# The reciprocal root of three layer normalisations as a power on GpSimd

## The chip, the cores and the metric

The kernel runs on one core of one Trainium2 chip. The metric is the device time of one execution in microseconds (us). The profile is of one more execution, taken by the hardware profiler; its times in the rows are us from the start of its span.

## The reference

The input x has shape 4 x 512 x 128 in float32, 2048 tokens of 128 features. Four blocks follow each other, each with a layer normalisation ahead of it and a residual addition behind it:

```
def _layernorm(x, axis=-1, eps=1e-05):
    m = jnp.mean(x, axis=axis, keepdims=True)
    v = jnp.var(x, axis=axis, keepdims=True)
    return (x - m) / jnp.sqrt(v + eps)

x = x + attn_a(_layernorm(x), ...)   # inner training, two steps
x = x + ffn(_layernorm(x), ...)      # mixture of 8 experts, the best 2
x = x + attn_b(_layernorm(x), ...)   # 16 heads, block-causal, own normalisation on top
x = x + ffn(_layernorm(x), ...)      # the same mixture again
```

In ffn a token's gates are a softmax over 8 logits; the two largest, made to sum to 1, weigh the outputs x We + be of their experts.

## The kernel before

The tokens lie in 16 tiles of 128 (partitions) x 128, all in the SBUF tensor x. The phases run one after the other, each a block in which every engine has an instruction list of its own, tied to the others by semaphores: qkv_phase, two rounds of gradient_phase and schulz_phase, query_phase (together the first block of the reference), moe_phase(0), attention_phase, moe_phase(1). The order on each engine is written out by hand; `pipeline` interleaves stages with a lag between them.

**The layer normalisation** is made for all 16 tiles at once. The statistics of each tile (L176, one instruction a tile) come at the end of the phase before. `ln_vector` on VectorE turns them into a variance plus epsilon in five steps of 128 x 16 (L182 to L186), each waiting for the one before; then it signals (L187), makes the mean in two steps (L188, L189), waits for the root (L190) and takes its reciprocal into rstd (L191). `ln_scalar` on ScalarE loads the Sqrt table (L195), waits for the variance and takes the root (L197). The first phase calls both as well and needs the Sqrt table for other roots too (L283, L306).

**moe_phase.** VectorE: L1138 is the normalisation, L1147 normalises a tile, in groups of four tiles; L1153 copies logits; from L1160 a long serial chain finds the two best gates (L1160, L1161 maximum and shift, L1163 to L1165 softmax, `best` twice, up to L1183, which writes the weights wt). TensorE turns the normalised tiles (L1096), makes logits (L1103) and turns those (L1109), waits for all logits to be copied (L1123), then runs `experts` for the first two tiles, twelve matmuls through `mm3` (L117 to L119, where each matmul's record stands), then in `weights` turns wt (L1115) and makes the twelve matmuls for the experts' biases (again L117 to L119), for which VectorE waits before its four additions to x (L1194, L1197). ScalarE: L1041 is `ln_scalar`; L1047 and L1052 copy tiles and logits; L1065 loads the Exp table; L1061 makes the high parts of the first two tiles, which GpSimd's low parts (L1034) and through them the experts wait for; L1070 is the exponential, which waits for the shifted logits (L1069). GpSimd begins with eight memsets of the priorities (L1014), copies tiles (L1021), makes low parts (L1034), then one half-sum per tile (L1030); VectorE goes on with L1212, L1217 and the addition to x at L1222.

**attention_phase.** ScalarE: L1370 is `ln_scalar`, L1371 loads Exp. GpSimd: memsets of the mask (L1343, L1346), then the bias (L1351). VectorE: L1514 is the normalisation, L1521 normalises four tiles, and TensorE turns them (L1412).

In the first phase GpSimd's list starts with memsets of ones, ident and be (L245, L246, L250); the last of them releases SP's loads of the expert biases (L602).

Of the kernel before, what the change touches and what calls it, by code (L numbers as in the profile page):

```python
# [29 lines left out]
P = 128  # L30
# [91 lines left out]
class Kernel:  # L122
    def __init__(self, nc, ctx, args, out):
        self.nc, self.ctx = nc, ctx
        self.a, self.out = args, out
        sb, ps = self.sb, self.ps
        self.x = sb("x", [P, NT, P])
        self.ident = sb("ident", [P, P])
        self.ones = sb("ones", [P, P])
        self.mean = sb("mean", [P, NT])  # L130
        self.rstd = sb("rstd", [P, NT])
        self.stats = sb("stats", [P, NT, 6])
        self.lnw = sb("lnw", [P, 4, NT])

        self.we = sb("we", [P, NE * P])
        self.weh, self.wel = sb("weh", [P, NE * P], F32R), sb("wel", [P, NE * P], F32R)
        self.wg, self.bg = sb("wg", [P, NE]), sb("bg", [NE, 1])

        self.beh, self.bel = sb("beh", [P, NT * P], F32R), sb("bel", [P, NT * P], F32R)

        self.wh, self.wl = sb("wh", [P, 3 * HEADS * DH], F32R), sb("wl", [P, 3 * HEADS * DH], F32R)
        self.wout, self.bout = sb("wout", [P, NP, P]), sb("bout", [P, 1, P])
        self.lng, self.lnb = sb("lng", [P, 1]), sb("lnb", [P, 1])
        self.s_late, self.s_bias, self.s_parts = self.sem("late"), self.sem("bias"), self.sem("parts")
        self.gradient_sems()
        self.schulz_sems()
# [28 lines left out]

        return e.bn_stats(self.stats[:, bass.ds(tile, 1), :], self.x[:, bass.ds(tile, 1), :])  # L176

    def ln_vector(self, e, s_var, s_root, s_ln):

        st, w = self.stats, self.lnw  # L180
        c = Chain(e, s_ln)
        c(e.tensor_tensor(w[:, 0, :], st[:, :, 1], st[:, :, 4], ALU.subtract))  # L182
        c(e.tensor_tensor(w[:, 1, :], w[:, 0, :], w[:, 0, :], ALU.mult))
        c(e.tensor_tensor(w[:, 2, :], st[:, :, 2], st[:, :, 5], ALU.add))
        c(e.scalar_tensor_tensor(w[:, 3, :], w[:, 1, :], P / 4.0, w[:, 2, :], ALU.mult, ALU.add))
        c(e.tensor_scalar(w[:, 3, :], w[:, 3, :], 1.0 / P, LN_EPS, ALU.mult, ALU.add))  # L186
        e.sem_inc(s_var, 1)  # L187
        c(e.tensor_tensor(w[:, 0, :], st[:, :, 1], st[:, :, 4], ALU.add))  # L188
        c(e.tensor_scalar(self.mean[:, :], w[:, 0, :], 0.5, None, ALU.mult))  # L189
        e.wait_ge(s_root, 1)  # L190
        c(e.reciprocal(self.rstd[:, :], w[:, 1, :]))  # L191
        return c.n

    def ln_scalar(self, e, s_var, s_root):
        e.preload_act_table(ACT.Sqrt)  # L195
# [5 lines left out]
    def qkv_phase(self):  # L201
# [8 lines left out]
        with ExitStack() as c:  # L210
# [32 lines left out]
            @block.gpsimd  # L243
            def _(pool):
                pool.memset(self.ones[:, :], 1.0).then_inc(s_cst, 1)  # L245
                pool.memset(ident[:, :], 0.0).then_inc(s_cst, 1)  # L246
                pool.wait_ge(s_cst, 2)
                pool.affine_select(out=ident[:, :], in_=ident[:, :], compare_op=ALU.not_equal, fill=1.0, base=0,
                                   pattern=[[-1, P]], channel_multiplier=1).then_inc(s_cst, 1)
                pool.memset(self.be[:, :, :], 0.0).then_inc(self.s_bias, 1)  # L250
                pool.wait_ge(s_cst, 3)
                pool.wait_ge(s_unit, 6 * 16)
                g = Chain(pool, s_pre)
                per_head = lambda ap, n: ap[:, n * P:n * P + P].rearrange("p (g d) -> p g d", d=QD)
                for dst, src in ((scale_all, scale), (shift_all, shift_)):
                    for n in range(2):
                        g(pool.tensor_tensor(per_head(dst, n), per_head(self.ones, 0), src[:, n:n + 1, :].broadcast_to([P, QH, QD]), ALU.mult))
                wide = lambda ap: ap.rearrange("p (a d) -> p a d", d=P)
                g(pool.tensor_tensor(wide(self.gvh[:, :]), wide(self.gv[:, :]),
                                     self.ones[:, :].unsqueeze(1).broadcast_to([P, 2 * NC, P]), ALU.mult))  # L260
                g(pool.tensor_tensor(self.gvl[:, :], self.gv[:, :], self.gvh[:, :].bitcast(F32), ALU.subtract))
                pool.wait_ge(s_ptc, 2)
                g(pool.tensor_tensor(self.pTl[:, :], self.projT[:, :], self.pTh[:, :].bitcast(F32), ALU.subtract))
                pool.sem_inc(s_s, 2)
                pool.sem_inc(s_b, 2)

                def unit(t):
                    pool.wait_ge(s_inv, t.done())
                    pool.wait_ge(s_s, t.done())
                    pool.tensor_tensor(m[:, t.ring, :].rearrange("p (g d) -> p g d", d=QD),  # L270
                                       qkv[:, tile(t), 0:2 * P].rearrange("p a (g d) -> p (a g) d", d=QD),
                                       inv[:, heads(t)].unsqueeze(2).broadcast_to([P, 2 * QH, QD]), ALU.mult).then_inc(s_m, 1)

                def scaled(t):
                    pool.wait_ge(s_m, t.done())
                    pool.wait_ge(s_b, t.done())
                    pool.tensor_tensor(sc[:, t.ring, :], m[:, t.ring, :], scale_all[:, :], ALU.mult).then_inc(s_s, 1)

                pipeline(pool, (0, unit), (1, scaled))()
# [66 lines left out]
            @block.vector  # L346
            def _(dve):
                for g in range(BATCH):
                    dve.wait_ge(s_x[g], 16)
                    for n in range(TPB):  # L350
                        self.take_stats(dve, g * TPB + n).then_inc(s_stat, 1)
                dve.wait_ge(s_stat, NT)
                self.ln_vector(dve, s_var, s_root, s_ln)
                dve.scalar_tensor_tensor(nmr[:, :], self.mean[:, :], -1.0, self.rstd[:, :], ALU.mult, ALU.mult).then_inc(s_shift, 1)
                dve.sem_inc(s_xT, 2)
                dve.sem_inc(s_out, 2)
                dve.sem_inc(s_ss, 2)
                dve.sem_inc(s_T, 2)
                dve.wait_ge(s_w, 32)
                dve.wait_ge(s_pre, 4)  # L360

                def bias_add(t):
                    dve.wait_ge(s_qkv, t.done())
                    dve.tensor_tensor(qkv[:, tile(t), :], psQ[t.ring][:, :], bias[:, :], ALU.add).then_inc(s_out, 1)

                def sumsq(t):
                    dve.wait_ge(s_sq, t.done())
                    dve.tensor_reduce(ssq[:, heads(t)], sq[:, t.ring, :].rearrange("p (g d) -> p g d", d=QD),
                                      AX.X, ALU.add).then_inc(s_ss, 1)

                def guard(t):
                    dve.wait_ge(s_rt, t.done())
                    dve.tensor_scalar(ssq[:, heads(t)], ssq[:, heads(t)], 1e-6, None, ALU.add).then_inc(s_gd, 1)

                def invert(t):
                    dve.wait_ge(s_gd, t.done())
                    dve.reciprocal(inv[:, heads(t)], ssq[:, heads(t)]).then_inc(s_inv, 1)

                def shift(t):
                    dve.wait_ge(s_s, t.done() + 2)  # L380
                    dve.wait_ge(s_T, t.done())
                    dve.wait_ge(s_k, t.done())
                    dve.tensor_tensor(u[:, t.ring, :], sc[:, t.ring, :], shift_all[:, :], ALU.add).then_inc(s_b, 1)

                pipeline(dve, (2, bias_add), (3, sumsq), (4, guard), (8, shift), (5, invert))()
# [199 lines left out]
    def load_later_weights(self, sp):  # L585
# [13 lines left out]
        ]  # L599
        for dst, src in loads:  # L600
            sp.dma_start(dst, src).then_inc(self.s_late, 16)
        sp.wait_ge(self.s_bias, 1)  # L602
        for t in range(NT):
            sp.dma_start(self.be[t * NE:(t + 1) * NE, t, :], self.a["L0_ffn_be"]).then_inc(self.s_late, 16)

# [363 lines left out]
    def moe_phase(self, nth):  # L969
# [13 lines left out]
        with ExitStack() as c:  # L983
# [26 lines left out]

            @block.gpsimd
            def _(pool):
                for n in range(NE):
                    last = pool.memset(prio[:, :, n:n + 1], float(NE - n))  # L1014
                last.then_inc(s_prio, 1)
# [22 lines left out]

            @block.scalar
            def _(act):  # L1040
                self.ln_scalar(act, s_var, s_root)  # L1041

                def copy(t):
                    act.wait_ge(s_xT, t.done() + 2)
# [17 lines left out]

                act.sem_inc(s_E, 2)
                act.sem_inc(s_w, 2)
                act.preload_act_table(ACT.Exp)  # L1065
                act.wait_ge(s_keep, 1 + 2)
                for t in FIRST:
                    high(t)
# [201 lines left out]
    def attention_phase(self):  # L1270
# [4 lines left out]
        with ExitStack() as c:  # L1275
# [63 lines left out]

            @block.gpsimd  # L1340
            def _(pool):
                g = Chain(pool, t["cst"])
                g(pool.memset(mask[:, :], 0.0))  # L1343
                for n in range(P // FRAME - 1):
# [22 lines left out]

            @block.scalar
            def _(act):
                self.ln_scalar(act, t["var"], t["root"])  # L1370
                act.preload_act_table(ACT.Exp)  # L1371

                def take_x(b):
# [281 lines left out]
```

## Time and profile before

| | us |
|---|---|
| median of 3 runs | 913.87 (912.15 to 914.26) |
| the profiled execution's own time | 913.51 |
| its span | 911.7 |
| TensorE, matmuls busy | 778.6 (85%) |
| TensorE, weight loads busy | 594.6 (65%) |
| VectorE busy | 600.5 (66%) |
| ScalarE busy | 420.7 (46%) |
| GpSimd busy | 376.6 (41%) |

In the rows PE is TensorE (PEld its weight loads), DVE VectorE, ACT ScalarE, POOL GpSimd, and L12 is line 12 of the kernel. Times at matmuls are modelled: an entry's duration has the pipeline's depth in it, and the spacing of starts tells the rate. A timeline row that stands for several instructions (x4) has the time from the first start to the last end. An idle time in brackets is that of the engine before the row, with what ended it. PEclk is the clock that TensorE was granted, 1.00 for 2.4 GHz and 0.50 for 1.2 GHz. The normalisations of the second, third and fourth block stand at about 406, 476 and 843 us.

### The profile page before, as it was taken

To read this page: it belongs to the slowest core of one execution; us is meant where nothing else is said; L and a number is where in the kernel's file an instruction comes from. 1 tells how busy PE (TensorE), PEld (TensorE's weight loads), DVE (VectorE), ACT (ScalarE), POOL (GpSimd) and SP (SyncE) were. 2 spreads that over 40 slices of the span, in tenths; PEclk is the share of its full clock that TensorE was granted. 3 is DMA by queue.
4 is the path that set the end of the run, shared out by engine and by line. 5 is a ranking of instruction groups with operands and counts; after the bars stand their busy time and mean duration, and the time that the engine had idled before them with its cause. 6 is when DMAs were issued, how large, how long until landed. Compare 5 with 4: busy or idle time off the path is not lost. (4 is left out here: it accounts for less than half of the span.)

```text
span 911.7 us, 16940 instructions
## 1 busy us (share of the span) xinstructions
PE 778.6 (85%) x5464; PEld 594.6 (65%) x5464; DVE 600.5 (66%) x1621; ACT 420.7 (46%) x1190; POOL 376.6 (41%) x512
## 2 busy tenths in 40 slices
PE   3669999879999667968628999999999999998763
PEld 1249999758999656755315766777777777777442
DVE  3936665355655556766996767766676666664698
ACT  4743332433333223314534666565556555562453
POOL 4854443015445534204642443343334333332275
PEclk9979999989999978997987999999999999999798
DMA  3030000000000000000000000000000000000001
GB/s 99 1 128 1 0 0 1 1 0 1 1 0 0 1 0 1 1 1 0 0 0 1 2 1 2 2 1 2 2 1 1 2 1 1 2 1 2 1 12 35
DMA packets 9327, 7.00 MB, mean 8 GB/s; under 512 B 1456, under 2 KB 8880, under 8 KB 9136
## 3 DMA queue, kind: packets, MB, share of 16 engines
q1 hardware_dynamic: 9264, 6.18, 2.1%
q8 instruction: 37, 0.61, 0.3%
q14 instruction: 26, 0.21, 0.1%
HBM read 5.13 MB, written 1.05 MB: 7 GB/s over the span
## 5 line engine op out<-in xcount | busy, mean ns | idle before, releaser
L1356 POOL TENSOR_SCALAR t_p_<-t_p_,t_rinv_ 128x128 f32<-128x128 f32 (+3 forms) x256 | 132.5, 535 | 213.5 <-DVE t_rinv_ L1551 213.5
L1544 DVE CUSTOM_DVE_ANT_0 t_p_<-t_S_,t_mask_ 128x128 f32<-128x128 f32 (+3 forms) x256 | 112.8, 487 | 72.7 <-PE t_S_ L1443 69.2
L1386 ACT ACTIVATE t_p_<-t_p_,t_nmin_ 128x128 f32<-128x128 f32 (+3 forms) x256 | 140.0, 551 | 9.0 <-DVE t_nmin_ L1544 9.0
L1391 ACT ACTIVATE t_pT_<-t_T_ 128x384 f32<-128x384 f32 (+1 forms) x96 | 50.7, 528 | 128.3 <-PE t_T_ L1455 128.3
L1455 PEld LDWEIGHTS t_T_<-ident,t_p_ 128*128 128x128 f32 x640 | 68.3, 140 | 44.6 <-POOL t_p_ L1356 28.7
L1443 PE MATMUL t_S_<-t_k_,t_q_ 64*128 64x256 f32 (+3 forms) x512 | 95.0, 469 | 0.0
L1470 PE MATMUL t_O_<-t_pT_,t_v_ 128*64 128x128 f32 x1280 | 91.0, 280 | 0.1
L1455 PE MATMUL t_T_<-ident,t_p_ 128*128 128x128 f32 x640 | 91.0, 281 | 0.0
L1470 PEld LDWEIGHTS t_O_<-t_pT_,t_v_ 128*64 128x64 f32 x1280 | 67.9, 136 | 29.9 <-ACT t_pT_ L1391 26.5
L432 POOL TENSOR_TENSOR g_sp<-g_s,g_t 128x512 f32<-128x512 f32 x32 | 40.9, 1277 | 103.3 <-DVE g_t L553 103.3
L1555 DVE COPY t_pT_<-t_T_ 128x384 f32<-128x384 f32 (+1 forms) x96 | 57.3, 597 | 3.1 <-PE t_T_ L1455 3.0
L544 DVE TENSOR_TENSOR g_sw<-g_G,g_s 128x512 f32<-128x512 f32 x32 | 22.1, 692 | 55.3 <-ACT g_s L456 55.3
L1030 POOL TENSOR_TENSOR m_z_<-m_y_ 128x512 f32<-128x512 f32 x32 | 43.4, 1355 | 27.9 <-DVE m_y_ L1204 27.9
L117 PE MATMUL m_E_<-weh,m_xh_ 128*128 128x512 f32 x64 | 29.2, 456 | 29.5 <-issue 14.9
L1443 PEld LDWEIGHTS t_S_<-t_k_,t_q_ 64*128 64x128 f32 x512 | 41.3, 185 | 18.9 <-issue 15.8
L1386 ACT ACTIVATION_READ_ACCUMULATOR t_p_<-t_p_,t_nmin_ 128x1 f32 x256 | 48.7, 190 | 0.0
L465 ACT ACTIVATE g_hT<-g_H 128x512 f32<-128x512 f32 x32 | 19.1, 597 | 58.3 <-PE g_H L497 58.3
L438 POOL TENSOR_TENSOR g_w<-g_u,g_sp 128x512 f32<-128x512 f32 x32 | 41.3, 1292 | 3.6 <-POOL g_sp L432 2.2
L1217 DVE TENSOR_TENSOR m_z_<-m_z_ 128x128 f32<-128x128 f32 x32 | 39.6, 1238 | 0.8 <-DVE x L1222 0.5
L117 PEld LDWEIGHTS m_E_<-weh,m_xh_ 128*128 128x128 f32 x64 | 13.0, 204 | 41.3 <-POOL m_xl_ L1034 19.9
L1083 ACT ACTIVATE m_y_<-m_E_,m_wt_ 128x128 f32<-128x128 f32 x128 | 36.4, 368 | 6.0 <-PE m_E_ L119 6.0
L504 PEld LDWEIGHTS g_PT<-proj,g_hT 128*128 128x128 f32 x256 | 33.6, 192 | 2.6
(270 smaller groups left out, 1849.4 us busy)
## 6 DMA issues: line engine op xcount, KB each, us to landing
wqkv<-in_L_attn_b_w_qkv_dram SPq DMA_DIRECT2D x1, 1536.0 KB
x<-in_L_attn_a_x_dram SPq DMA_DIRECT2D x4, 256.0 KB, 4.0
out_dram<-x SPq DMA_DIRECT2D x4, 256.0 KB, 2.3
we<-in_L_ffn_We_dram SPq DMA_DIRECT2D x1, 512.0 KB
wout<-in_L_attn_b_w_out_dram SPq DMA_DIRECT2D x1, 512.0 KB
proj<-n_L_attn_a_ttt_proj_dram SPq DMA_DIRECT2D x1, 256.0 KB, 6.1
gv<-n_L_attn_a_ttt_gate_dram SPq DMA_DIRECT2D x1, 256.0 KB, 5.1
gv<-in_L_attn_a_ttt_val_dram SPq DMA_DIRECT2D x1, 256.0 KB, 5.7
```

What stands on the lines that cost most here:

```text
L117: e.matmul(out, ah, bh, start=start, stop=False)
L432: pool.tensor_tensor(sp_[:, t.ring, :], s_[:, t.ring, :], t1[:, t.ring, :], ALU.subtract).then_inc(g["sp"], 1)
L438: pool.tensor_tensor(w1[:, t.ring, :], u_[:, t.ring, :], sp_[:, t.ring, :], ALU.mult).then_inc(g["w1"], 1)
L1030: pool.tensor_tensor(z[:, t.ring, :], y[:, t.ring, 0:4 * P], y[:, t.ring, 4 * P:8 * P], ALU.add).then_inc(s_z, 1)
L1356: last = pool.tensor_scalar(pr[:, G.par, h, cols], pr[:, G.par, h, cols], rinv[:, G.par, n:n + 1], 1.0, ALU.mult, ALU.mult)
L1386: act.activation(pr[:, G.par, h, cols], pr[:, G.par, h, cols], ACT.Exp, bias=nmin[:, G.par, n:n + 1], scale=-1.0, accum_out=rsum[:, G.par, ...
L1391: act.activation(pT[:, G.par, 0, G.blocks], psT[:, 0, 0:G.width], ACT.Copy).then_inc(t["eA"], 1)
L1443: last = pe.matmul(psS[:, (2 * G.n + h) % 3, at_:at_ + (qt + 1) * P], qp[d, G.par, qt * P:qt * P + P], kp[d, G.par, 0:(qt + 1) * P], start ...
L1455: last = pe.transpose(psT[:, h, k:k + P], pr[:, G.par, h, at_:at_ + P], ident[:, :])
L1470: last = pe.matmul(psO[d, qt * P:qt * P + P], v[:, G.b % 2, n, G.p * P + h * DH:G.p * P + h * DH + DH], pT[:, G.par, h, at_:at_ + P], star ...
L1544: dve.tensor_tensor_reduce(pr[:, G.par, h, cols], psS[:, (2 * G.n + h) % 3, at_:at_ + keys], mask[:, SEQ - keys:SEQ], 1.0, -NEG, ALU.add, ...
L1555: dve.tensor_copy(pT[:, G.par, 1, G.blocks], psT[:, 1, 0:G.width]).then_inc(t["eB"], 1)
```

## The change

The root and the reciprocal of the three later normalisations become one instruction on GpSimd, `tensor_tensor` with the operation pow: variance plus epsilon to the power -0.5, the exponent coming from a new tensor mhalf that is filled once at the start. GpSimd does it ahead of its other work in each of the three blocks. The first normalisation stays as it was. ScalarE no longer loads Sqrt in the three blocks; in moe_phase its Exp load moves from behind the logits to the head of the list, in attention_phase it alone remains.

```diff
--- before.py
+++ after.py
@@ -131,6 +131,7 @@
         self.rstd = sb("rstd", [P, NT])
         self.stats = sb("stats", [P, NT, 6])
         self.lnw = sb("lnw", [P, 4, NT])
+        self.mhalf = sb("mhalf", [P, NT])
 
         self.we = sb("we", [P, NE * P])
         self.weh, self.wel = sb("weh", [P, NE * P], F32R), sb("wel", [P, NE * P], F32R)
@@ -175,7 +176,7 @@
 
         return e.bn_stats(self.stats[:, bass.ds(tile, 1), :], self.x[:, bass.ds(tile, 1), :])
 
-    def ln_vector(self, e, s_var, s_root, s_ln):
+    def ln_vector(self, e, s_var, s_root, s_ln, by_power=True):
 
         st, w = self.stats, self.lnw
         c = Chain(e, s_ln)
@@ -188,8 +189,13 @@
         c(e.tensor_tensor(w[:, 0, :], st[:, :, 1], st[:, :, 4], ALU.add))
         c(e.tensor_scalar(self.mean[:, :], w[:, 0, :], 0.5, None, ALU.mult))
         e.wait_ge(s_root, 1)
-        c(e.reciprocal(self.rstd[:, :], w[:, 1, :]))
+        if not by_power:
+            c(e.reciprocal(self.rstd[:, :], w[:, 1, :]))
         return c.n
+
+    def ln_power(self, pool, s_var, s_root):
+        pool.wait_ge(s_var, 1)
+        pool.tensor_tensor(self.rstd[:, :], self.lnw[:, 3, :], self.mhalf[:, :], ALU.pow).then_inc(s_root, 1)
 
     def ln_scalar(self, e, s_var, s_root):
         e.preload_act_table(ACT.Sqrt)
@@ -243,6 +249,7 @@
             @block.gpsimd
             def _(pool):
                 pool.memset(self.ones[:, :], 1.0).then_inc(s_cst, 1)
+                pool.memset(self.mhalf[:, :], -0.5).then_inc(self.s_bias, 1)
                 pool.memset(ident[:, :], 0.0).then_inc(s_cst, 1)
                 pool.wait_ge(s_cst, 2)
                 pool.affine_select(out=ident[:, :], in_=ident[:, :], compare_op=ALU.not_equal, fill=1.0, base=0,
@@ -350,7 +357,7 @@
                     for n in range(TPB):
                         self.take_stats(dve, g * TPB + n).then_inc(s_stat, 1)
                 dve.wait_ge(s_stat, NT)
-                self.ln_vector(dve, s_var, s_root, s_ln)
+                self.ln_vector(dve, s_var, s_root, s_ln, by_power=False)
                 dve.scalar_tensor_tensor(nmr[:, :], self.mean[:, :], -1.0, self.rstd[:, :], ALU.mult, ALU.mult).then_inc(s_shift, 1)
                 dve.sem_inc(s_xT, 2)
                 dve.sem_inc(s_out, 2)
@@ -599,7 +606,7 @@
         ]
         for dst, src in loads:
             sp.dma_start(dst, src).then_inc(self.s_late, 16)
-        sp.wait_ge(self.s_bias, 1)
+        sp.wait_ge(self.s_bias, 2)
         for t in range(NT):
             sp.dma_start(self.be[t * NE:(t + 1) * NE, t, :], self.a["L0_ffn_be"]).then_inc(self.s_late, 16)
 
@@ -1010,6 +1017,7 @@
 
             @block.gpsimd
             def _(pool):
+                self.ln_power(pool, s_var, s_root)
                 for n in range(NE):
                     last = pool.memset(prio[:, :, n:n + 1], float(NE - n))
                 last.then_inc(s_prio, 1)
@@ -1038,7 +1046,7 @@
 
             @block.scalar
             def _(act):
-                self.ln_scalar(act, s_var, s_root)
+                act.preload_act_table(ACT.Exp)
 
                 def copy(t):
                     act.wait_ge(s_xT, t.done() + 2)
@@ -1062,7 +1070,6 @@
 
                 act.sem_inc(s_E, 2)
                 act.sem_inc(s_w, 2)
-                act.preload_act_table(ACT.Exp)
                 act.wait_ge(s_keep, 1 + 2)
                 for t in FIRST:
                     high(t)
@@ -1339,6 +1346,7 @@
 
             @block.gpsimd
             def _(pool):
+                self.ln_power(pool, t["var"], t["root"])
                 g = Chain(pool, t["cst"])
                 g(pool.memset(mask[:, :], 0.0))
                 for n in range(P // FRAME - 1):
@@ -1367,7 +1375,6 @@
 
             @block.scalar
             def _(act):
-                self.ln_scalar(act, t["var"], t["root"])
                 act.preload_act_table(ACT.Exp)
 
                 def take_x(b):
```

## Rows read from the trace of the kernel before

**Rows 1.** The profile's page, its first line.

```profile
span 911.7 us, 16940 instructions
```

**Rows 2.** Timeline, second block's normalisation: start us, us, engine, line, operation [idle before].

```profile
406.04 1.28 ACT L195 ACT_TABLE_LOAD   x1 [7.85 <-PEq L854]
...
406.93 0.17 DVE L186 TENSOR_SCALAR lnw<-lnw 128x16 f32<-128x16 f32 x1
407.25 0.18 DVE L188 TENSOR_TENSOR lnw<-stats 128x16 f32<-128x16 f32 x1 [0.15 <-DVE lnw L186]
407.33 0.22 ACT L197 ACTIVATE lnw<-lnw 128x16 f32<-128x16 f32 x1
407.47 0.17 DVE L189 TENSOR_SCALAR mean<-lnw 128x16 f32<-128x16 f32 x1
407.68 0.25 DVE L191 RECIPROCAL rstd<-lnw 128x16 f32<-128x16 f32 x1
408.66 2.14 DVE L1147 TENSOR_SCALAR m_xn_<-x,mean,rstd 128x128 f32<-128x128 f32 x8 [0.73 <-DVEq L1139]
```

**Rows 3.** Timeline, attention block: the last normalised tile and its reader on GpSimd.

```profile
478.11 1.11 DVE L1521 TENSOR_SCALAR t_xn_<-x,mean,rstd 128x128 f32<-128x128 f32 x4
...
479.37 1.26 POOL L1351 TENSOR_TENSOR x<-x,bout 128x512 f32<-128x512 f32 x1 [2.07 <-DVE t_xn_ L1521]
```

**Rows 4.** Groups by form, GpSimd: line, engine, operation, shapes, count | busy us, mean ns | idle.

```profile
L1034 POOL TENSOR_TENSOR m_xl_<-m_xnT_,m_xh_ 128x128 fp32r<-128x128 f32 x32 | 15.5, 488 | 20.4 <-ACT m_xh_ L1061 20.4
...
L1021 POOL TENSOR_TENSOR m_xnT_<-m_xTs_,ones 128x512 f32 x8 | 10.1, 1267 | 13.1 <-ACT m_xTs_ L1047 13.1
```

**Rows 5.** Groups by form, VectorE, same columns.

```profile
L1217 DVE TENSOR_TENSOR m_z_<-m_z_ 128x128 f32<-128x128 f32 x32 | 39.6, 1238 | 0.8 <-DVE x L1222 0.5 <-issue 0.3
...
L544 DVE TENSOR_TENSOR g_sw<-g_G,g_s 128x512 f32<-128x512 f32 x32 | 22.1, 692 | 55.3 <-ACT g_s L456 55.3
```

**Rows 6.** Chain of work that ended last, fourth block: start us, us, what.

```profile
855.49 1.28 ACT L1065
856.79 0.51 ACT m_xh_ L1061 x2
857.53 0.30 DVE m_tot_ L1163
```

**Rows 7.** Timeline, second block, from its logits to its bias.

```profile
419.00 1.28 ACT L1065 ACT_TABLE_LOAD   x1
...
420.03 0.29 DVE L1161 TENSOR_TENSOR m_logit_<-m_logit_,m_m_ 128x128 f32<-128x128 f32 x1
420.30 0.51 ACT L1061 ACTIVATE m_xh_<-m_xnT_ 128x128 fp32r<-128x128 f32 x2
420.69 0.87 POOL L1034 TENSOR_TENSOR m_xl_<-m_xnT_,m_xh_ 128x128 fp32r<-128x128 f32 x2 [2.59 <-ACT m_xh_ L1061]
420.71 0.29 ACT L1070 ACTIVATE m_gate_<-m_logit_ 128x128 f32<-128x128 f32 x1
...
421.24 0.76 PE L117 MATMUL m_E_<-weh,m_xh_ 128*128 128x512 f32 x1 [1.79 <-issue]
...
426.07 0.63 PE L119 MATMUL m_E_<-weh,m_xl_ 128*128 128x512 f32 x1
...
427.03 0.33 PE L1115 MATMUL m_T_<-ident,m_wt_ 128*128 128x128 f32 x1 [0.34 <-DVE m_wt_ L1183]
...
428.12 0.50 PE L117 MATMUL m_T_<-beh,m_wTh_ 128*128 128x512 f32 x1 [0.76 <-DVE m_wTl_ L1192]
...
430.77 0.39 PE L119 MATMUL m_T_<-beh,m_wTl_ 128*128 128x512 f32 x1
...
431.20 0.69 DVE L1197 TENSOR_TENSOR x<-m_T_,x 128x512 f32<-128x512 f32 x1 [1.95 <-PE m_T_ L119]
```

**Rows 8.** Windows, second block: stretch, length, busy by engine (instructions), PE's granted clock.

```profile
404.20:406.30 2.10, 0.00 (x0) 0.00 (x0) 1.74 (x7) 0.26 (x1) 0.27 (x6) 1.00 0.00 0
406.40:409.80 3.40, 0.00 (x0) 0.00 (x0) 2.34 (x12) 1.14 (x2) 0.08 (x2) 0.50 0.02 5
```

## The prediction, made before the changed kernel had run

> **What bounds the kernel now.** I began with the page: one core, a span of 911.7 us [rows 1] inside a profiled execution of 913.51 us. That execution lies 0.36 us under the median of the three runs shown, which spread over 2.1 us; 0.3%, about what a measurement of this kernel can tell from no change, is 2.7 us. No engine is the bound all through, so a saving counts only if it lies on the path at its own place. The change touches three short serial stretches (second, attention and fourth block), and I read these in the timeline, then the chain of waits, then the costs of GpSimd.
>
> The normalisation [rows 2]: VectorE makes the variance, last step L186, done at 407.10. ScalarE, whose Sqrt table was being loaded from 406.04 to 407.32, takes the root at 407.33 and is done at 407.55. But VectorE is busy itself with the mean (L188, L189) until 407.64, so its reciprocal at 407.68 starts behind its own mean, not behind ScalarE. The reciprocal ends at 407.93; 0.73 us of VectorE's own sequencing follow before the first normalised tile at 408.66. The table load before the root is thus already hidden: it ends just in time. The other two places repeat this.
>
> The second table load is the one that shows. In the chain of the fourth block it stands as a link: L1065 for 1.28 us, then two high parts of 0.51 us, then the softmax sum [rows 6]. The second block has the same order [rows 7]: Exp table from 419.00 to 420.28, high parts at 420.30, exponential at 420.71, while its input (L1161) was ready at 420.32.
>
> **The change, term by term.** Times are differences at one place, minus is a gain.
>
> *The reciprocal root, three places.* Gone from the path: the reciprocal. In its place stands VectorE to GpSimd, the power, GpSimd to VectorE. Start: the signal leaves between L186 and L188, at about 407.2; GpSimd starts about 0.15 us behind a VectorE result (the normalised tile ends at 479.22, its reader starts at 479.37) [rows 3]; so 407.35, and I take 407.4 since L188 is running then. Duration: no row shows a power on GpSimd. From below: additions take 488 ns for 128 columns and 1267 ns for 512 [rows 4], 2.03 ns a column, so 16 columns of plain arithmetic would be 0.26 us. From above within the nearest rows: the whole 512-column addition, 1.27 us, which is 32 times the columns. Between: the same function costs 0.22 (root) plus 0.25 (reciprocal) [rows 2], and GpSimd needs 1267 ns where VectorE needs 692 for one shape [rows 4, 5], a factor 1.83: 0.86 us, which I take because it is the only value that rests on this function. With 0.1 us back to VectorE the result is there at 407.4 + 0.86 + 0.1 = 408.36, against 407.93: +0.43. Bounds: 407.76 gives -0.17, 408.77 gives +0.84. Nothing else covers it: VectorE waits with nothing but the tiles behind it, and TensorE, ScalarE and GpSimd wait for the tiles. Three places: **+1.3** (-0.5 to +2.5).
>
> *One rule bears on this.* The row first: VectorE additions of two SBUF operands with 128 columns take 1238 ns on average where GpSimd's halving sum runs beside them [rows 5], and 0.29 us where it doesn't, as at L1161 [rows 7]. So VectorE is held until GpSimd's instruction ends. L188 reads two SBUF operands. It should be ahead of the power, and L189 (a single operand) ends long before it.
> The Trainium skill ("SBUF — State Buffer", the section on the two separate sides) says the port pair shared by these engines is an exclusive lock, and against a GpSimd instruction that reads SBUF it binds a VectorE operation with two SBUF inputs. The trace agrees, by the 1238 ns; the rule speaks against this change, and its price is the third rival.
>
> *Sqrt loads, three.* Hidden as shown, nothing is won. If I misread that, the cover is VectorE's two mean operations and the gain is under the 0.1 us between 407.55 and 407.64.
>
> *Exp load moved to the head of the MoE blocks.* It runs while VectorE computes the variance, from 406.04 for 1.28 us; ScalarE's next work is on transposed tiles, and no tile is normalised before 408.66 [rows 2], so it is hidden. In the attention block Exp alone is loaded, earlier than now; ScalarE next works after the tiles are transposed. At the old place 1.28 us vanish from ScalarE's queue: high parts at 419.0, GpSimd's low parts from 419.39 to 420.26 instead of 420.69 to 421.56 [rows 7]. L1161, due at 420.03, now meets the second low part and ends about 0.14 us behind it, at 420.41 instead of 420.32. The exponential then starts at 420.45 instead of 420.71. Gain 0.26, not 1.28: VectorE's reduction of the logits is next in line. Two places: **-0.5** (0 to -0.7).
>
> *What the early high parts do to TensorE.* The first two tiles' twelve expert matmuls start at 419.94 instead of 421.24. Before, they ran at the 1.2 GHz level, spaced (426.07 - 421.24) / 11 = 0.44 us, and ended at 426.70, 0.33 us ahead of the next TensorE work at 427.03, the transpose of the gate weights, which waits for VectorE; the twelve bias matmuls then ran at 2.4 GHz, spaced (430.77 - 428.12) / 11 = 0.24 us [rows 7]. After, TensorE ends at 422.9 (if it runs at 2.4 GHz) or 425.4 (if not), and idles until 426.8, for 1.4 to 3.9 us. Elsewhere 2.2 us of idleness took the clock from 1.00 to 0.50: TensorE did nothing from 404.2 and the clock is at 0.50 from 406.4 on [rows 8]. So the bias matmuls may run at 1.2 GHz: 12 x 0.20 = 2.4 us. Nothing covers that, since VectorE has been idle 1.95 us at 431.20 for their end [rows 7] and works without a break from there. Bounds 0 and 2.4 us a block. I take 0.6: the fall depends on when the idle time comes, the clock can rise again during the bias work, and the kernel before must pay it too in executions less lucky than this one. Two blocks: **+1.2** (0 to +4.8).
>
> *On GpSimd*, the memsets (priorities, mask) wait for the variance and the power, some 2 us later at most. Their readers come later still: priorities are read after the logits, from 420 on, the mask at the first scores, and GpSimd's own next work needs tiles that are normalised, turned and copied. The new memset at the start covers 16 columns, beside loads of several us. SP waits for it too, by a count of 2, before the bias loads, but the other memset it waits for is the later one. Nothing.
>
> Sum: 1.3 - 0.5 + 1.2 = +2.0 us on 913.51, 915.5; most of the 0.36 us by which the median stands above the profiled run added, **915.8 us**, no measurable difference.
>
> **The rivals.**
> 1. *Quick power, clock stays.* 0.26 us of power and no fall: -0.5 - 0.5 = -1.0, 912.5 to 912.9. For it: tiny operand. Against: software on GpSimd is the slower engine in every row. A gain over 2.7 us has no source at all: at its lower bounds all terms together give -1.9 us (-0.5, -1.4). 12 in 100, faster by more than 0.3% 5 in 100.
> 2. *TensorE's clock falls in both MoE blocks*, in most executions: 1.3 - 0.5 + 4.8 = +5.6, 919.1, slower. It decides once more than about 1 us a block is paid. For it: idle of up to 3.9 us against 2.2 seen to suffice. Against: the rise during the bias work. 15 in 100.
> 3. *The lock catches the mean.* If GpSimd gets its port first, L188 and L189 run behind the power, about 0.3 us more at each place: +0.9, 916.7. 6 in 100.
> 4. *A long power.* Break-even is 0.43 us; above 1.1 us a power the three places cost over 2 us and with the other terms the kernel is slower. At 3 us: 3 x 2.57 + 0.7 = +8.4, 922. For it: a power is no basic arithmetic, and nothing in the trace bounds it. 18 in 100.
> The forecast itself (within 0.3%) has 49 in 100, of which some 5 would come out above 2.7 us. A further way, that the tables would still be loaded, is unlikely: every load in the trace stands at a line that asks for one.
>
> **Numbers.** Faster 0.05; slower 0.15 + 0.18 + 0.05 = 0.38; same 0.57. The range goes from rival 1 with some spread, 912.3, to 921.0, which takes in the clock's full price and a power of some 2.5 us. The forecast's own range is 913.0 to 916.6.
>
> **What would show it.** The power's row: 0.86 us, start 0.25 to 0.3 us behind L186's end, three of them. Gap from L186's end to the first tile (L1147): 1.56 us before, 2.0 after. No load at the softmax; the exponential 0.26 us earlier against the last logits. First expert matmul 0.5 us behind the logits' transposes instead of 1.8. TensorE's clock and spacing in the bias matmuls: 0.24 or 0.44. Wrong, if the power is over 1.1 or under 0.4 us, or if the clock during the bias work is the same as before in several executions.

## The result, and the profile after

The changed kernel takes 921.95 us (median of 4 runs, 921.17 to 923.25) against 914.07 for the kernel before (now four runs, 912.15 to 914.3): a ratio of 1.0092, with a 95% interval of 1.0074 to 1.0110. It is slower by 7.9 us. Forecast were 915.8 us and no measurable difference, with a range up to 921.0: wrong, and outside the range. A second comparison, told of below, gave 1.0094 (1.0061 to 1.0127).

The page of the changed kernel begins, against [rows 1]:

```profile
span 920.4 us, 16929 instructions
```

The timeline of its second block (line numbers are 1 higher than before in `ln_vector`, 7 or 8 in moe_phase), for [rows 2]:

```profile
405.34 1.28 ACT L1049 ACT_TABLE_LOAD   x1 [7.85 <-PEq L861]
405.37 0.19 DVE L183 TENSOR_TENSOR lnw<-stats 128x16 f32<-128x16 f32 x1 [0.30 <-PEq L861]
...
406.23 0.17 DVE L187 TENSOR_SCALAR lnw<-lnw 128x16 f32<-128x16 f32 x1
406.54 2.91 POOL L198 TENSOR_TENSOR rstd<-lnw,mhalf 128x16 f32<-128x16 f32 x1 [35.87 <-DVEq L188]
406.56 0.24 DVE L189 TENSOR_TENSOR lnw<-stats 128x16 f32<-128x16 f32 x1 [0.15 <-DVE lnw L187]
406.84 0.17 DVE L190 TENSOR_SCALAR mean<-lnw 128x16 f32<-128x16 f32 x1
409.41 0.44 POOL L1022 MEMSET m_prio_<- 128x16 f32 x8
410.17 2.14 DVE L1154 TENSOR_SCALAR m_xn_<-x,mean,rstd 128x128 f32<-128x128 f32 x8 [3.15 <-DVEq L1146]
```

The variance is ready at 406.40, and GpSimd starts 0.14 us behind it: the hand-over is as short as was taken. The power then runs for **2.91 us**. VectorE has its mean by 407.0 and waits with nothing to do; the first normalised tile comes 0.72 us behind the power's end, the same sequencing of its own as before. From the first step of the normalisation (L183) to the first normalised tile it is 4.80 us, against 2.59 before, where the first step is this row:

```profile
406.07 0.18 DVE L182 TENSOR_TENSOR lnw<-stats 128x16 f32<-128x16 f32 x1 [0.30 <-PEq L854]
```

The other two places have the same power. The groups of GpSimd, by form, give the mean of the three, and the chain of waits of the fourth block has it as a link where the reciprocal stood:

```profile
L198 POOL TENSOR_TENSOR rstd<-lnw,mhalf 128x16 f32<-128x16 f32 x3 | 8.7, 2916 | 54.4 <-DVEq L188 54.4
```

```profile
848.50 2.93 POOL rstd L198
```

The timeline of the second block from its high parts to its bias, for [rows 7] (L1167 is the first step of the chain, the logits' maximum):

```profile
420.88 0.49 ACT L1069 ACTIVATE m_xh_<-m_xnT_ 128x128 fp32r<-128x128 f32 x2
...
421.25 0.87 POOL L1042 TENSOR_TENSOR m_xl_<-m_xnT_,m_xh_ 128x128 fp32r<-128x128 f32 x2 [1.17 <-ACT m_xh_ L1069]
...
421.70 0.29 DVE L1167 TENSOR_REDUCE m_m_<-m_logit_ 128x16 f32<-128x128 f32 x1
421.80 0.47 PE L117 MATMUL m_E_<-weh,m_xh_ 128*128 128x512 f32 x1 [0.37 <-DVE m_logit_ L1160]
...
422.02 0.29 DVE L1168 TENSOR_TENSOR m_logit_<-m_logit_,m_m_ 128x128 f32<-128x128 f32 x1
...
422.35 0.31 ACT L1077 ACTIVATE m_gate_<-m_logit_ 128x128 f32<-128x128 f32 x1 [0.98 <-DVE m_logit_ L1168]
...
422.69 0.28 DVE L1170 TENSOR_REDUCE m_tot_<-m_gate_ 128x16 f32<-128x128 f32 x1 [0.38 <-ACT m_gate_ L1077]
...
424.41 0.40 PE L119 MATMUL m_E_<-weh,m_xl_ 128*128 128x512 f32 x1
...
428.68 0.33 PE L1122 MATMUL m_T_<-ident,m_wt_ 128*128 128x128 f32 x1 [3.88 <-DVE m_wt_ L1190]
...
429.77 0.79 PE L117 MATMUL m_T_<-beh,m_wTh_ 128*128 128x512 f32 x1 [0.76 <-DVE m_wTl_ L1199]
...
433.83 0.39 PE L119 MATMUL m_T_<-beh,m_wTl_ 128*128 128x512 f32 x1
...
434.26 0.69 DVE L1204 TENSOR_TENSOR x<-m_T_,x 128x512 f32<-128x512 f32 x1 [3.35 <-PE m_T_ L119]
```

In the kernel before, the first step of the chain is here:

```profile
419.71 0.29 DVE L1160 TENSOR_REDUCE m_m_<-m_logit_ 128x16 f32<-128x128 f32 x1
```

Exp is no longer loaded here. The exponential starts 0.04 us behind its input instead of 0.39, and the softmax sum (L1170) 0.99 us behind the first step of the chain instead of 1.33. But TensorE starts its expert matmuls at 421.80, has started the last of the twelve at 424.41, and has 3.88 us of nothing until the gate weights are there, which its transpose L1122 waits for. Its bias matmuls then take (433.83 - 429.77) / 11 = 0.37 us each instead of 0.24, and VectorE waits for them 3.35 us instead of 1.95. In the fourth block TensorE is idle for only 2.31 us ahead of that transpose, and VectorE waits 4.38 us instead of 1.96:

```profile
869.70 0.46 PE L1122 MATMUL m_T_<-ident,m_wt_ 128*128 128x128 f32 x1 [2.31 <-DVE m_wt_ L1190]
...
876.44 0.69 DVE L1204 TENSOR_TENSOR x<-m_T_,x 128x512 f32<-128x512 f32 x1 [4.38 <-PE m_T_ L119]
```

The windows of the same kernel (length, busy times, TensorE's granted clock) show why, as [rows 8] did elsewhere:

```profile
425.00:428.60 3.60, 0.00 (x0) 0.00 (x0) 3.22 (x12) 0.00 (x0) 0.00 (x0) 1.00 0.00 0
428.60:429.10 0.50, 0.33 (x1) 0.14 (x1) 0.03 (x1) 0.00 (x0) 0.00 (x0) 1.00 0.00 0
429.70:432.80 3.10, 3.03 (x7) 2.45 (x8) 1.21 (x3) 2.29 (x9) 2.27 (x4) 0.50 0.00 0
869.70:870.20 0.50, 0.46 (x1) 0.16 (x1) 0.00 (x0) 0.00 (x0) 0.00 (x0) 0.55 0.00 0
870.80:874.20 3.40, 3.29 (x8) 2.61 (x9) 1.25 (x3) 2.32 (x10) 2.54 (x4) 0.50 0.01 2
```

In the second block TensorE does nothing from 425.0 to 428.6, still at a clock of 1.00, and its transpose of the gate weights at 428.68 still runs at 1.00. By the bias matmuls, from 429.77 on, the clock is 0.50, which is 1.2 GHz; it comes back at 432.8, behind the seventh of them. In the fourth block the clock falls during the transpose and doesn't come back before the bias matmuls are done.

Where the time went. Each figure is a stretch between two starts in the timeline after, less the same stretch in the timeline before:

| stretch | second block | attention | fourth block | sum |
|---|---|---|---|---|
| first step of the normalisation to the first normalised tile | +2.21 | +2.30 | +2.22 | +6.73 |
| first tile to the logits' maximum | +0.48 | | -0.39 | +0.09 |
| maximum to the softmax sum | -0.34 | | -0.34 | -0.68 |
| softmax sum to the gate weights | 0.00 | | +0.01 | +0.01 |
| gate weights to VectorE's bias additions | +1.41 | | +2.46 | +3.87 |

That is 10.0 us, where the spans differ by 8.7. The rest lies in stretches that the change doesn't touch: 0.7 us ahead of the second block, 0.6 in the attention's body. The kernel before moves by as much between executions: over all experiments it took between 909.8 and 918.7 us. What makes it do so ahead of the MoE blocks was not looked into, and is why each verdict below is a ratio with its interval.

### The profile page after: what moved, and what is told of

Its sections match the earlier page's. It is cut to its first block and busy times, and to the rows that moved or that the text cites. A ratio compares the mean times of both kernels' runs of the same rounds, so it can differ in the third digit from the quotient of the medians.

```text
span 920.4 us, 16929 instructions
## 1 busy us (share of the span) xinstructions
PE 777.6 (84%) x5462; PEld 594.4 (65%) x5464; DVE 599.9 (65%) x1618; ACT 415.8 (45%) x1184; POOL 385.0 (42%) x516
```

## The experiments

**The power's length against the trip to GpSimd.** In the changed kernel, one word:

```diff
-self.mhalf[:, :], ALU.pow).then_inc(s_root, 1)
+self.mhalf[:, :], ALU.mult).then_inc(s_root, 1)
```

> The changed kernel with mult instead of pow in GpSimd's instruction, same operands, so rstd is the variance times -0.5 and the output is another. Theory (the length of the power itself is the loss): the instruction takes about 0.26 us instead of 2.92, the first normalised tile comes 1.5 us or less behind the variance, and the kernel is some 7.5 us faster than the changed one, 914 to 915.5. Rival (the trip to GpSimd and back is the loss): the instruction is short but at least 1 us of waiting stays at each of the three places, 917 or more.

Measured: 1.0019 of the kernel before (0.9994 to 1.0044). The timeline of its second block:

```profile
408.28 0.22 POOL L198 TENSOR_TENSOR rstd<-lnw,mhalf 128x16 f32<-128x16 f32 x1 [36.91 <-DVEq L188]
...
408.57 0.34 DVE L190 TENSOR_SCALAR mean<-lnw 128x16 f32<-128x16 f32 x1
409.66 1.11 DVE L1154 TENSOR_SCALAR m_xn_<-x,mean,rstd 128x128 f32<-128x128 f32 x4 [0.75 <-DVEq L1146]
```

GpSimd's instruction takes 0.22 us, and the first tile comes 2.56 us behind the first step of the normalisation, against 4.80 with the power and 2.59 with ScalarE's root and VectorE's reciprocal. The attention block has 1.92 (1.90 before), the fourth 2.30 (2.20). So the trip costs at most 0.1 us, and the power's length is the loss at the normalisations: the rival falls. 1.0092 - 1.0019 is 0.73%, 6.7 us, the sum of the ledger's first line. There is a second reading: even with an instruction of 0.22 us nothing is won over the kernel before. At the normalisations the path is VectorE's own steps (and the mean, L190, took 0.34 us beside GpSimd's memsets, where it took 0.17 in the changed kernel). What early Exp wins at the softmax, 0.34 and 0.33 us, is more than lost behind it: this kernel's bias additions waited 3.66 us in the second block and 4.38 in the fourth, as in the changed kernel:

```profile
434.95 0.69 DVE L1204 TENSOR_TENSOR x<-m_T_,x 128x512 f32<-128x512 f32 x1 [3.66 <-PE m_T_ L119]
```

**What a power costs.** Six more instructions in GpSimd's idle time ahead of the second block, among them:

```diff
+pool.tensor_tensor(prb[:, 0:4], lhs[:, 0:4], half[:, 0:4], ALU.pow)
+pool.tensor_tensor(prb[:, 4:20], lhs[:, 0:16], half[:, :], ALU.pow)
+pool.tensor_tensor(prb[:, 36:100], lhs[:, 0:64], lhs[:, 0:64], ALU.pow)
```

> The changed kernel with six more GpSimd instructions in the idle time ahead of the second block: pow of 4, 16 and 64 columns of constants, pow of the 16 variances with the exponent -0.5 and with ones, mult of 16 columns. They lie in idle time, so the time doesn't move by more than 1 us. Theory (the power costs per element): 4 columns 0.9 us, 16 columns 2.9, 64 columns 11, whatever the data; mult 0.26. Rival (a fixed cost, code or set-up): all near 2.9 us. Second rival (it depends on the data): the constants' 16 columns differ from the variances'.

Its groups of GpSimd by form (L881 to L885 are powers, L886 is the product):

```profile
L884 POOL TENSOR_TENSOR q_prb_<-ones 128x64 f32<-128x64 f32 x1 | 10.5, 10512 | 0.0
...
L882 POOL TENSOR_TENSOR q_prb_<-ones,mhalf 128x16 f32<-128x16 f32 x1 | 2.9, 2897 | 0.0
L883 POOL TENSOR_TENSOR q_prb_<-lnw,mhalf 128x16 f32<-128x16 f32 x1 | 2.9, 2892 | 0.0
L885 POOL TENSOR_TENSOR q_prb_<-lnw,ones 128x16 f32<-128x16 f32 x1 | 2.9, 2892 | 0.0
...
L881 POOL TENSOR_TENSOR q_prb_<-ones,mhalf 128x4 f32<-128x4 f32 x1 | 1.4, 1355 | 0.1
...
L886 POOL TENSOR_TENSOR q_prb_<-lnw,mhalf 128x16 f32<-128x16 f32 x1 | 0.2, 215 | 0.0
```

One execution took 924.5 us, 2.6 above the changed kernel's median, where at most 1 was expected. The changed kernel's own executions lie within 2.1 us, those of the kernel before within 9, and one execution can't tell; in the trace the six instructions are over by 392.1 and GpSimd is idle for 16.12 us before the normalisation's power, so they don't lie on the path. The durations are the answer. From 4 to 16 columns a column costs (2897 - 1355) / 12 = 128 ns, from 16 to 64 it is (10512 - 2897) / 48 = 159 ns; back to no columns the first slope leaves about 0.84 us. So it is both a fixed part and a price per column, and neither theory alone had it: at 64 columns the estimate of 11 held, at 4 columns 0.9 was too low. At 16 columns the data tried make no difference: ones and variances, exponents -0.5 and 1, all 2.89 to 2.90. A product of the same 16 columns takes 0.215, a thirteenth.

**The power cut in four.** 

```diff
+for g in range(BATCH):
+    n = slice(g * TPB, g * TPB + TPB)
+    pool.tensor_tensor(self.rstd[:, n], self.lnw[:, 3, n], self.mhalf[:, n], ALU.pow).then_inc(s_root, 1)
...
+dve.wait_ge(s_root, t.done())
```

> The changed kernel with the power cut into four instructions of 4 columns, and each group of four tiles waiting only for its own. Theory (the power costs by the column and only its end holds the path): the first group's power takes 1.36 us instead of 2.92, the first normalised tile of each block comes 1.5 us sooner, and the later groups, which are 1.1 us apart and more, follow; 3 to 4.5 us faster than the changed kernel. Rival (GpSimd's running power holds VectorE's normalisation as its additions do): the later three powers, 1.33 us each, stretch the normalised tiles, and little or nothing is won.

Measured: 1.0055 (1.0035 to 1.0075), median 919.15, with the changed kernel at 922.81 in the same comparison: 3.7 us won. Its second block:

```profile
408.07 4.04 POOL L200 TENSOR_TENSOR rstd<-lnw,mhalf 128x4 f32<-128x4 f32 x4 [36.87 <-DVEq L188]
...
409.88 2.14 DVE L1157 TENSOR_SCALAR m_xn_<-x,mean,rstd 128x128 f32<-128x128 f32 x8 [1.36 <-DVEq L1148]
...
412.20 2.13 DVE L1157 TENSOR_SCALAR m_xn_<-x,mean,rstd 128x128 f32<-128x128 f32 x4 [0.18 <-PE m_T_ L1105]
```

From the first step of the normalisation to the first tile it is 2.97, 2.34 and 2.67 us now, 0.4 to 0.5 above the kernel before and 1.8 below the changed one. And the eight normalised tiles take 2.14 us beside the running powers, as in [rows 2] with GpSimd idle. The rival falls: a power on GpSimd does not hold VectorE. Of the 5.4 us won at the three first tiles, 1.5 are gone again by the logits' maximum. In the second block that stretch is 12.09 us instead of 11.53, and TensorE's clock comes back to 1.00 more than 6.1 us behind the first tile, where in the changed kernel it took less than 5.8. In the fourth it is 11.93 instead of 10.96: the second eight tiles take 5.20 us instead of 4.13, beside GpSimd's products.

**Early Exp alone**, in the kernel before: the root as it was, Exp right behind it.

```diff
 self.ln_scalar(act, s_var, s_root)
+act.preload_act_table(ACT.Exp)
...
-act.preload_act_table(ACT.Exp)
 act.wait_ge(s_keep, 1 + 2)
```

> The kernel before with one part of the change: Exp loaded behind the root at the head of both MoE blocks, no power. Theory (the clock is a cost of this part): the softmax sum starts 0.99 us behind the logits' maximum instead of 1.33, so -0.34 us a block; but the twelve expert matmuls start some 1.3 us earlier, TensorE idles 2 to 4 us before the gate weights come, and in many executions the twelve bias matmuls run at 1.2 GHz. Together +0.5 to +3 us against the kernel before, with executions that differ by a few us. Rival (the clock is chance and costs both kernels the same): -0.7 us.

Measured: 1.0023 (1.0004 to 1.0043), slower by 2.1 us. The softmax sum is 0.34 us earlier in both blocks, as meant, and yet:

```profile
426.47 0.79 PE L117 MATMUL m_T_<-beh,m_wTh_ 128*128 128x512 f32 x1 [0.76 <-DVE m_wTl_ L1192]
...
431.33 0.63 PE L119 MATMUL m_T_<-beh,m_wTl_ 128*128 128x512 f32 x1
...
432.00 0.69 DVE L1197 TENSOR_TENSOR x<-m_T_,x 128x512 f32<-128x512 f32 x1 [4.38 <-PE m_T_ L119]
```

Bias matmuls of (431.33 - 426.47) / 11 = 0.44 us, and VectorE idle for 4.38 us; 3.67 us in the fourth block. The part of the change that was to win time loses it: 2.1 + 0.7 = 2.8 us for the clock, 1.4 us a block. In this one profiled execution the stretch from the gate weights to the bias additions is longer by more, 2.45 and 1.76 us. TensorE was idle for 2.31 us before the gate weights in the second block and for 3.88 in the fourth.

**The power with Exp where it was.** The changed kernel with the load back behind the logits.

> The changed kernel with the Exp load at its old place behind the logits. Theory: the power's 6.7 us stay, the softmax sum is 0.34 us later in two blocks, and TensorE has no long idle time before the gate weights, so the bias matmuls mostly run at 2.4 GHz: 920 to 921, some 1 to 2 us under the changed kernel. Rival (the clock is chance): 0.7 us above the changed kernel, 922.6.

Measured: 1.0047 (1.0025 to 1.0070). The second block:

```profile
421.65 1.28 ACT L1071 ACT_TABLE_LOAD   x1
...
430.76 0.50 PE L117 MATMUL m_T_<-beh,m_wTh_ 128*128 128x512 f32 x1 [0.76 <-DVE m_wTl_ L1198]
...
433.86 0.69 DVE L1203 TENSOR_TENSOR x<-m_T_,x 128x512 f32<-128x512 f32 x1 [1.96 <-PE m_T_ L119]
```

VectorE waits 1.96 us there and 1.97 in the fourth block, both at a granted clock of 1.00, and the normalisations keep their 4.79, 4.21 and 4.42 us. Against the changed kernel this is 0.47% less, 4.3 us, more than the 1 to 2 expected; the ledger has 3.87 - 0.68 = 3.2 for it, and the intervals take in both. None of its ten executions took over 921.6 us, and eight of them took less than any of the changed kernel's eight (921.17 and more).

**TensorE kept busy.** The changed kernel with ten matmuls into a free bank, each behind one step of VectorE's chain:

```diff
 if t.number() == 0:
+    for k in range(10):
+        pe.wait_ge(s_ln, 17 + k)
+        pe.matmul(psT[:, 0, :], weh[:, 0:P], weh[:, 0:SEQ], start=True, stop=True)
     pe.wait_ge(s_c, 1)
```

> The changed kernel with ten added matmuls of 512 columns into a free bank, one behind each of the last ten steps of VectorE's gate chain, so that TensorE isn't idle before the gate weights. Theory (idleness brings the clock down in the bias matmuls): their spacing is 0.23 us in both blocks, and VectorE's idle time before its bias additions is about 1.95 us instead of 3.35 and 4.38; 1.5 to 3.5 us faster than the changed kernel, 918.5 to 920.5. Rival (the clock falls whatever TensorE does there): same as the changed kernel or slower by the added matmuls.

Measured: 1.0048 (1.0024 to 1.0072), 4.2 us under the changed kernel. VectorE's wait is 1.95 us in both blocks, here the second:

```profile
433.99 0.69 DVE L1207 TENSOR_TENSOR x<-m_T_,x 128x512 f32<-128x512 f32 x1 [1.95 <-PE m_T_ L119]
```

All ten executions (914.56 to 921.06) lie under all eight of the changed kernel. Added work whose result nobody reads makes the kernel faster. With the early experts and every other part of the change as they were, only TensorE's idleness was taken away, and the clock stayed at 1.00 during the bias: this is the run that shows the mechanism.

**Early Exp with the experts held back.** Early Exp alone, and TensorE waits for the softmax sum before its experts:

```diff
 pe.wait_ge(s_l, BATCH + 2)
+pe.wait_ge(s_ln, 10)
```

> The kernel before with Exp loaded early, but TensorE waits with its expert matmuls for the softmax sum, so that it starts them where it starts them now, against VectorE's chain. Theory: the gain of 0.34 us a block without the idle time: -0.7 us against the kernel before, 913.4, and 1 to 3 us under the run with early experts. Rival (no clock effect): the same time as that run.

Measured: 1.0001 (0.9977 to 1.0026). TensorE's timeline:

```profile
418.05 0.77 PE L117 MATMUL m_E_<-weh,m_xh_ 128*128 128x512 f32 x1 [1.64 <-DVE m_tot_ L1164]
...
424.77 0.50 PE L117 MATMUL m_T_<-beh,m_wTh_ 128*128 128x512 f32 x1 [0.76 <-DVE m_wTl_ L1193]
```

The experts run late, as before, and the bias at 2.4 GHz: VectorE's wait for it is 1.95 us in both blocks. In the trace the loss of early Exp is gone; in time the two runs differ by 0.22%, and their intervals overlap. The 0.7 us don't show within an interval of 0.5%.

**Early Exp and TensorE kept busy**, in the kernel before:

> The kernel before with Exp loaded early, experts early, and ten added matmuls behind the last ten steps of the gate chain. Theory: TensorE at 2.4 GHz in the bias matmuls in every execution, -0.7 us from the chain and what the kernel before itself loses in its less lucky executions, about 1 us a block: 911.5 to 913.5. Rival (no clock effect): -0.7 us or 0, like the run without the added matmuls.

Measured: 0.9978 (0.9957 to 0.9998). The ten added matmuls, the first bias matmul and VectorE's wait:

```profile
421.90 3.27 PE L1116 MATMUL m_T_<-weh 128*128 128x512 f32 x10 [0.79 <-DVE m_gate_ L1180]
...
426.08 0.51 PE L117 MATMUL m_T_<-beh,m_wTh_ 128*128 128x512 f32 x1 [0.76 <-DVE m_wTl_ L1195]
...
429.18 0.69 DVE L1200 TENSOR_TENSOR x<-m_T_,x 128x512 f32<-128x512 f32 x1 [1.95 <-PE m_T_ L119]
```

Since the interval only just excluded no gain, once more:

> The kernel with the reciprocal root as before, Exp early and the ten added matmuls once more, since its first interval (0.9957 to 0.9998) only just excludes no gain. Theory (0.34 us a block from the softmax, and the clock kept): 0.1 to 0.3% faster than the kernel before again. Rival (the first result was the spread of the kernel before): a ratio within 0.1% of 1.

Measured: 0.9976 (0.9959 to 0.9994). This version beats both kernels, by 2.1 us over the one before. The chain gives 0.7 us of it; the theory puts the rest down to executions in which the kernel before loses the clock as well. The one profiled execution of the kernel before does not do so in these two places (1.95 and 1.96 us of waiting), so this second part is argued and not shown. The next run was to test it by itself and does not bear it out.

**The added matmuls alone**, with Exp behind the logits:

> The kernel before with the ten added matmuls alone; Exp stays behind the logits. Theory (the kernel before also loses the clock in some executions): 0 to 2 us faster than the kernel before, by executions, and the bias matmuls at 0.23 us. Rival: the gain of the run with early Exp and added matmuls was all of early Exp; then this is the same as the kernel before.

Measured: 1.0017 (1.0001 to 1.0034), slower by 1.6 us; neither the theory nor the rival had that.

```profile
430.42 0.50 PE L117 MATMUL m_T_<-beh,m_wTh_ 128*128 128x512 f32 x1 [0.76 <-DVE m_wTl_ L1195]
...
433.51 0.69 DVE L1200 TENSOR_TENSOR x<-m_T_,x 128x512 f32<-128x512 f32 x1 [1.95 <-PE m_T_ L119]
```

The bias ran at 2.4 GHz and VectorE's wait was 1.95 us, but from the gate weights (427.07) to the bias additions it is 6.44 us instead of 4.51: TensorE had started its experts late and slowly, until 426.9, and was in its added matmuls when the weights came. In the fourth block it is 5.42 instead of 4.63. Work that keeps the clock has to end in time; with early experts it does. And since this run pays for the overshoot, it doesn't tell whether the kernel before loses the clock in some executions: that stays open.

**The changed kernel again**, beside these:

> The changed kernel unchanged, beside the kernel before once more, since the kernel before spread over 7 us in the runs of the experiments so far. If the profile's ledger holds (6.7 us of normalisations, -0.7 of softmax, 1 to 2 us of clock), the difference is 7 to 8 us, 0.75 to 0.9%. If the executions of the first comparison were lucky ones of the kernel before, it is nearer 5 us.

Measured: 1.0094 (1.0061 to 1.0127), median 922.81. Its normalisations take 4.79, 4.20 and 4.42 us, VectorE's waits for the bias 3.40 and 4.39: the ledger repeats.

## Why the prediction was wrong

**The power's duration was the step that failed.** It was put at 0.86 us, by scaling ScalarE's root and VectorE's reciprocal with GpSimd's handicap in another operation, and bounded by 1.27 us, an instruction of 512 columns. It takes 2.91 us, so that the term at the three normalisations was +6.7 us instead of +1.3. This step alone takes the forecast out of its range: 915.8 with 5.4 us more is 921.2. The rows that the prediction calls additions are a product with ones (L1021, 1267 ns) and a subtraction (L1034), and VectorE's 692 ns is a product with one operand in PSUM. The bound was none: a product of 16 columns takes 0.215 us on GpSimd, a power of the same size thirteen times as long. The prediction had said so itself under its fourth rival ("nothing in the trace bounds it") and yet used 1.27 as the end of the term. That rival's condition came true, and its time was nearly exact: for 3 us it gave +8.4 and 922, measured were 2.91 us, +7.9 and 921.95. That it was so near is in part luck: it had 7.7 us for the powers, where 6.7 were paid, and 0.7 us for all the rest, where the profile has 3.2. It had 18 chances in 100 and lay at 922, a microsecond beyond the range's end at 921, which stopped at a power of 2.5 us.

**Hand-over and cover were right.** 0.15 us from VectorE to GpSimd was taken, 0.14 measured. The break-even at 0.43 us was too low, since the start was taken 0.16 us too late and 0.1 us added for the way back, which doesn't show in the MoE blocks (0.72 us from the result to the first tile, 0.73 before) and is 0.07 in the attention block: 2.91 us should have cost 2.48 by the formula and cost 2.2 to 2.3. That no Sqrt load would be won was right, as the product shows.

**Exp: right in sign and near in size.** -0.26 us a block was forecast and -0.34 measured; the exponential follows its input by 0.04 us. The low parts on GpSimd, which were to hold the chain for 0.14 us, did not (L1168 started beside them and took 0.29 us, as alone).

**The clock: mechanism right, size too small.** 0.6 us a block was taken out of 0 to 2.4. The profile has 1.41 and 2.46, the run with Exp early alone 1.4 on average, the run with TensorE kept busy 4.2 us for both blocks. The idle time came as worked out (3.88 and 2.31 us where 1.4 to 3.9 was said), and the bias matmuls at 1.2 GHz with it. What [rows 8] showed once, a fall after 2.2 us of idleness, is no measure: in the second block the clock was still 1.00 after 3.88 us of it, and fell 0.7 us later. With the terms repaired the sum is 6.7 - 0.7 + 2.8 = 8.8 us, or 10.2 with the clock at 4.2, over the 7.9 and 8.6 (1.0094) measured. What takes the 1 to 2 us back is not shown.

**The lock rival** didn't occur: L189, which reads two SBUF operands, started 0.02 us behind the power and took 0.24 us. Its price was worked out from an average beside additions, and doesn't hold for a power.

## What to carry to other kernels

An operation that the trace doesn't show has no price in the trace: its neighbours on the same engine did not bound it here (1.27 us for a product of 512 columns, 2.91 for a power of 16), so the range has to stay open. Before an instruction moves from one engine to another, multiply its columns with that engine's price for this very function, and start the waiting tiles on the first part of the result if it must stay. And an edit that lets TensorE begin earlier, but not end the wait behind its work, can hand the gain to the clock: ask what TensorE does between the early work and the next link of the chain.

## What the runs showed of the hardware

- A float32 power on GpSimd: 1.36 us for 128 x 4, 2.90 for 128 x 16, 10.5 for 128 x 64, at 16 columns the same for ones and for variances; in a queue of four of 4 columns each takes 4.04 / 4 = 1.0 us. A product of 128 x 16: 0.22.
- VectorE's normalised tiles, which GpSimd's products of 128 x 512 (L1021) stretch from 0.33 to 1.36 us, run undisturbed beside GpSimd's powers. The Trainium skill ("SBUF — State Buffer", the section on the two separate sides) has the port pair locked for the whole GpSimd instruction; the additions agree with it (1238 ns against 290 in [rows 5, 7]), the powers do not (eight tiles in 2.14 us beside them, and L189 with its two SBUF inputs in 0.24 us beside one of 2.91), and the measurement decides.
- TensorE was idle for 3.88 us with the clock at 1.00 all the while, ran one transpose still at 1.00, and had a clock of 0.50 at 429.77, 1.1 us behind the gap. In the fourth block 2.31 us of idleness was enough, with the fall during the transpose. The fall comes late enough to hit the work behind the gap, not the gap.
- Ten matmuls whose result nobody reads made a kernel 4.2 us faster.
